# A two-layer mixture of experts in one kernel: second choices chained behind first choices, rows that carry the residual, and shared units moved between the lists

## The reference, cut

```python
x = x + gnn0(layernorm(x), adj)        # eigenvectors U of the 64 x 64 normalised Laplacian of adj
#   agg = U.T @ features; out = U @ (relu(agg @ W1 + b1) @ W2 + b2)
x = x + ffn0(layernorm(x))
#   probs = softmax(x @ router.T); top 2 of 8 experts, gates normalised
#   out = sum over both: gate_e * ((silu(x @ w1_e.T) * (x @ w3_e.T)) @ w2_e.T)     hidden 341
x = x + gnn1(layernorm(x), adj)
#   A_hat mixes the 64 nodes; relu(batchnorm(agg @ W1.T + b1)) @ W2.T + b2, batchnorm   hidden 256
x = x + ffn1(layernorm(x))
#   shared = gelu(x @ W1s + b1s) @ W2s + b2s                                       hidden 512
#   top 2 of 8: gate_e * (gelu(x @ W1p_e + b1p_e) @ W2p_e + b2p_e), plus shared    hidden 512
```

## Time and profile before

| what | value |
|---|---|
| median of three runs | 1467.68 us (1464.34 to 1473.49) |
| the profiled execution | 1468.22 us, span 1466.4 us |
| busy, share of the span | PE 77%, DVE 62%, POOL 45%, ACT 38% |
| mean granted TensorE clock | 0.922 |
| DMA over the span | 125.58 MB, mean 86 GB/s |
| first instruction of the experts to the last, layer 0 | 442.2 to 802.2 us |
| the same, layer 1 | 1093.3 to about 1431 us |

### The profile page before, as it was taken

The page is one execution under the profiler, slowest core; times in us unless marked ns, Lnnn a source line. Parts: engine busy times, 40 slices in busy tenths (PEclk is TensorE's granted clock), DMA queues, the critical chain, the costliest instruction groups (busy, mean ns, idle before and its releaser), DMA issues.

```text
span 1466.4 us, 24078 instructions
## 1 busy us (share of the span) xinstructions
PE 1125.4 (77%) x6500; PEld 934.2 (64%) x6500; DVE 902.9 (62%) x3796; ACT 550.2 (38%) x1613; POOL 653.2 (45%) x675
## 2 busy tenths in 40 slices
PE   4555686388727978899999677999878877799990
PEld 3555575266615856688888443776657766699990
DVE  5776789767763544456676778887614433355673
ACT  3556567045511211122222365554323322244440
POOL 3000000054566666665444840044546666656664
PEclk9999999999958998899999798899989988899995
DMA  9993000001112222222242600011112222222436
GB/s 230 428 427 146 1 1 1 0 1 34 37 48 70 72 63 62 64 65 60 84 119 70 229 18 15 5 34 33 39 45 66 68 62 64 62 68 70 131 104 229
DMA packets 59270, 125.58 MB, mean 86 GB/s; under 512 B 13132, under 2 KB 39637, under 8 KB 57600
## 3 DMA queue, kind: packets, MB, share of 16 engines
q0 software_dynamic: 20000, 73.21, 13.2%
q1 hardware_dynamic: 39136, 50.84, 12.9%
HBM read 50.83 MB, written 74.99 MB: 86 GB/s over the span
## 4 chain that ended last, share of the span: by engine, by line
PE 48%; issue 32%; another core or an unknown queue 7%; DVE 6%; ACT 2%; DMA 2%; SPq 2%; POOL 1%; DVEq 0%; POOLq 0%; ACTq 0%
PE bank L1619 15%; PE bank L1610 9%; PE bank L1608 6%; PE bank L1607 6%; PE bank L1828 3%; PE bank L1836 3%; PE bank L1787 2%; PE bank L1595 2%; DMA u<-planes 1%; DVE bnh L1684 1%; PE bank L861 1%; SPq L2148 1%; DVE bn L1123 1%; ACT pay L1903 1%
## 5 line engine op out<-in xcount | busy, mean ns | idle before, releaser
L1462 POOL DMA_INDIRECT planes<-work,goal x284 | 300.9, 1059 | 211.0 <-DVE work L1531 124.2
L1016 POOL DMA_INDIRECT rows<-pay,slot x256 | 257.7, 1007 | 245.4 <-issue 78.3
L1619 PE MATMUL bank<-pay 128*128 128x128 f32 (+1 forms) x1988 | 297.7, 290 | 66.1 <-issue 34.0
L1619 PEld LDWEIGHTS bank<-pay 128*128 128x128 f32 (+1 forms) x1988 | 272.4, 199 | 95.3 <-issue 44.4
L1579 ACT ACTIVATE pay<-bank,pay 128x256 f32<-128x256 f32 x284 | 127.1, 475 | 211.3 <-PE bank L1610 123.9
L1575 ACT ACTIVATE pay<-bank 128x256 f32<-128x256 f32 (+1 forms) x213 | 81.1, 383 | 301.7 <-PE bank L1608 224.1
L1610 PE MATMUL bank<-pay 128*128 128x256 f32 x568 | 145.5, 402 | 3.0 <-issue 1.6
L1552 DVE TENSOR_TENSOR pay<-pay,bank 128x256 f32<-128x256 f32 (+1 forms) x213 | 88.6, 418 | 86.6 <-ACT pay L1575 44.5
L1607 PE MATMUL bank<-pay 128*128 128x256 f32 (+1 forms) x426 | 134.2, 398 | 7.6 <-issue 7.0
L1608 PE MATMUL bank<-pay 128*128 128x256 f32 (+1 forms) x426 | 131.7, 392 | 0.0
L195 PE MATMUL bank<-u 63*64 63x2 f32 (+61 forms) x496 | 73.7, 255 | 67.2 <-DVE u L180 66.1
(11 more groups left out here) (416 smaller groups left out, 2013.2 us busy)
## 6 DMA issues: line engine op xcount, KB each, us to landing
rows<-pay POOLq DMA_DIRECT2D x10, 3432.0 KB, 56.3
pay<-rows SPq DMA_DIRECT2D x142, 130.0 KB
u<-planes SPq DMA_DIRECT2D x64, 256.0 KB, 5.0
planes<-work,goal POOLq DMA_INDIRECT x284
wreg<-in_w SPq DMA_DIRECT2D x1, 4264.0 KB, 24.4
wreg<-in_w SPq DMA_DIRECT2D x1, 4112.0 KB, 13.3
X<-in_x SPq DMA_DIRECT2D x2, 2048.0 KB, 20.0
rows<-pay,slot POOLq DMA_INDIRECT x256
```

Source lines behind the costliest of these rows:

```text
L1016: return self.nc.gpsimd.indirect_dma_start(out=xs, out_offset=bass.IndirectOffsetOnAxis(ap=self.t["slot"][:, k, q:q + 1], axis=0), in_=sel ...
L1462: nc.gpsimd.indirect_dma_start(out=planes, out_offset=bass.IndirectOffsetOnAxis(ap=t["goal"][:, j * 2 + h:j * 2 + h + 1], axis=0), in_=t[" ...
L1619: ins = T.matmul(ps[4 + j % 2][:, h * P:(h + 1) * P], t["hh"][c][0:n, h * P:(h + 1) * P], t["wst"][j % 2][0:n, at + c * P:at + (c + 1) * P ...
```

## The change

First and second choices become two lists of 36 tiles (`LIST`), which run one after the other. A row now carries more: 128 features of the residual `X`, the 128 normalised features, and four numbers (token's number, both gates, and the slot of the token's second choice in `rows`, `AT_NEXT`); 260 floats. `finish` adds the gated result to the residual in the row itself (in `xin`, a ring of eight). For the first list POOL sends the whole row on to the slot of the second choice; for the second list it sends the 128 features to the token's place in `plane` (layer 0) or directly in `out` (layer 1). The second list's slots are filled from the upper end of each expert's room downwards. So there are no second sends and no planes to add.

Each list has 25 pure tiles and 11 split ones, whose two halves of 128 rows may have different experts: two weight sets are copied, up-products are done by halves, ACT does two gelus for one. Weight buffers are four (`WAYS`). SP waits at the start of the second list until every row of the first has been returned. In layer 1 the last 16 shared units (`HELD` = 2 token tiles) run on PE between the lists, and `RATE` is 5. The shared result of the first eight token tiles (`EARLY`) is added to `X` before these are sent; for the other eight ACT keeps it (`keep_shared`), and after the lists only these eight are fetched from `out`, added and stored again. The zero fill is twice as large, 20 blocks, and the wait for it moves from DVE at the start of graph layer 0 to ACT ahead of the first row of `first_norm_apply`.

```diff
-NT = (2 * TOKENS + E8 * (TS - 1)) // TS
+PURE = -(-(TOKENS - E8 * (TS - 1)) // TS)
+MIXED = (TOKENS + E8 * (P - 1)) // P - 2 * PURE
+MIXED += MIXED % 2
+LIST = PURE + MIXED // 2
+SETS = PURE + MIXED
+NT = 2 * LIST
+NS = 2 * SETS
-ROW = P + 2
+ROW = P + 4
+AT_ID, AT_G2, AT_G1, AT_NEXT = range(P, P + 4)
+FULL = P + ROW
-BLOCKS = 10
-RING = 18
-ZERO = E8 * CAP * ROW // (P * BLOCKS)
+BLOCKS = 20
+RING = 8
+WAYS = 4
+ZERO = E8 * CAP * FULL // (P * BLOCKS)
...
     if q == 0:
         act.wait_ge(*E.at("l1_scale"))
+        act.wait_ge(S("cleared"), 16 * BLOCKS)
...
     V.tensor_copy(t["rows"], ps[6][:, 0:1]).then_inc(S("a0_rows_out"), 1)
-    dve.wait_ge(S("cleared"), 16 * BLOCKS)
...
     for j in range(NT):
-        if route.split and j == PURE:
-            sp.wait_ge(S("route_sent_second"), 16 * N * sum(SPLIT[:layer + 1]))
-        at = sp.value_load(t["first"][j:j + 1, 0:1], min_val=0, max_val=E8 * CAP - TS)
-        if j >= 4:
-            sp.wait_ge(s("t"), past("t", j - 3))
-            sp.wait_ge(s("goal"), past("goal", j - 3))
-            sp.wait_ge(s("ys"), past("ys", j - 3))
...
+        if j == LIST:
+            for r in range(RING):
+                sp.wait_ge(s(f"back{r}"), past(f"back{r}", 32 * uses(r, LIST)))
...
+        if j >= RING:
+            sp.wait_ge(s(f"back{j % RING}"), past(f"back{j % RING}", 32 * (j // RING)))
+        if split(j):
+            for h in range(2):
+                sp.dma_start(t["xin"][j % RING][:, h, :], xs[bass.ds(ats[h], P), :]).then_inc(s(f"xin{j % RING}"), 16)
+        else:
+            sp.dma_start(t["xin"][j % RING], xs[bass.ds(ats[0], TS), :].rearrange("(p h) c -> p h c", h=2)
+                         ).then_inc(s(f"xin{j % RING}"), 16)
...
+    for j in range(NT):
+        out, width, column, last = (xs, FULL, P + AT_NEXT, E8 * CAP - 1) if j < LIST else (result, P, P + AT_ID, TOKENS - 1)
+        if split(j):
+            pool.wait_ge(s("goal"), past("goal", splits_before(j) + 1))
         pool.wait_ge(s("ys"), past("ys", j + 1))
         for h in range(2):
...
             nc.gpsimd.indirect_dma_start(
+                out=out, out_offset=bass.IndirectOffsetOnAxis(ap=goal, axis=0), in_=t["xin"][j % RING][:, h, 0:width],
+                in_offset=None, bounds_check=last, oob_is_err=False).then_inc(s(f"back{j % RING}"), 16)
...
-            for q in range(FREE + k * SENDS, min(N, FREE + (k + 1) * SENDS)):
-                route.send(q, 1, xs).then_inc(S("route_sent_second"), 16)
-            if k >= BEHIND:
-                give_back(j)
-                j += 1
...
-        if j >= RING:
-            dve.wait_ge(s("freed"), past("freed", j - RING + 1))
-        V.tensor_tensor(t["ysb"][j % RING], y, gate, ALU.mult).then_inc(s("ys"), 1)
+        gate = P + (AT_G1 if j < LIST else AT_G2)
+        for h in range(2):
+            ins = V.scalar_tensor_tensor(out=row[:, h, 0:P], in0=y[:, h, :], scalar=row[:, h, gate:gate + 1],
+                                         in1=row[:, h, 0:P], op0=ALU.mult, op1=ALU.add)
+        ins.then_inc(s("ys"), 1)
...
+        if j + 1 == LIST:
+            finish(j)
...
+                if split(j):
+                    A.activation(t["hh"][c][:, 0:P], ps[c][:, 0:P], ACT.Gelu, bias=bias[0])
+                    A.activation(t["hh"][c][:, P:TS], ps[c][:, P:TS], ACT.Gelu, bias=bias[1]).then_inc(s("hh"), 1)
...
+        if layer == 1 and j == LIST - 1:
+            for n in range(AHEAD, UNITS):
+                shared_act(nc, act, S, t, ps, n)
+                if n % (2 * CH1) == 2 * CH1 - 1:
+                    keep_shared(nc, act, S, t, ps, n // (2 * CH1))
...
+        for k, set_no in enumerate(sets_of(j)):
+            w = t["wst"][set_no % WAYS]
+            to = slice(k * P, (k + 1) * P) if split(j) else slice(0, TS)
+            ins = T.matmul(ps[c][0:n, to], w[:, a:a + n], x[:, to], start=True, stop=True)
...
+        if j + 1 == LIST:
+            if layer == 1 and HELD:
+                pe.wait_ge(s("ys"), past("ys", LIST - 1))
+                for n in range(AHEAD, UNITS):
+                    shared_pe(nc, pe, S, t, ps, n)
+                pe.wait_ge(S("a1_kept"), TILES - EARLY)
+            turn_in(LIST)
...
+def fetch_rows(sp, S, t, result, layer, tiles):
+
+    for r in range(RING):
+        sp.wait_ge(S(f"tile_back{r}"), 32 * uses(r, NT) * (layer + 1))
+    for T in tiles:
+        qs = slice(T * PAIRS, (T + 1) * PAIRS)
+        sp.dma_start(t["X"][:, qs, :], result[:, qs, :]).then_inc(S(f"rows{layer}_{T}"), 16)
...
-RATE = 6
+RATE = 5
+EARLY = 8
+HELD = 2
 UNITS = 2 * CH1 * TILES
-A1_STEPS = 2 + -(-UNITS // RATE)
+AHEAD = UNITS - 2 * CH1 * HELD
+A1_STEPS = 2 + -(-AHEAD // RATE)
+IN_ORDER = (0, 1, 2, 4, 3, 5, 6, 7)
...
     def ready(g):
         pool.wait_ge(S("a1_xh"), GT * (g + 1))
+        if GT * g < EARLY:
+            pool.wait_ge(S("a1_xsh"), GT * (g + 1))
 
     def rest(g, k):
-        if g + 1 < GROUPS:
-            pool.wait_ge(S("a1_hh"), RATE * g + (13, 14, 16)[k - 1])
-    for g in range(GROUPS):
+        if GT * (g + 1) < EARLY:
+            pool.wait_ge(S("a1_hh"), CH1 * GT * (g + 1) + (1, 2, 4)[k - 1])
+    for g in IN_ORDER:
         route.scatter(pool, g, xs, ready, rest)
...
+LATE = range(EARLY, TILES)
...
-    for T in range(TILES):
+    for T in LATE:
         qs = slice(T * PAIRS, (T + 1) * PAIRS)
-        pool.wait_ge(S("late_add"), TILES + T + 1)
+        pool.wait_ge(S("whole"), T - EARLY + 1)
         pool.dma_start(out[:, qs, :], t["X"][:, qs, :]).then_inc(S("stored"), 16)
```

More of the change, by code:

```diff
@@ L826 @@
               picked=GROUPS, gates=GROUPS, total=1, limits=1, limit_row=1, first=1)
-SENT = [16 * N if split else 32 * N for split in SPLIT]
+SENT = 16 * N
 def due(s, lag):
@@ L910, in choose @@
         dve.wait_ge(own.sem, n)
[L911 to L914, removed]
+        n = 2 * E8 * GQ
+        marks, i, e = r["o"], r["i"], r["e"]
         n = own.inc(V.tensor_tensor_scan(i, self.K[:, K_RESET:K_RESET + n], marks, 0.0, ALU.mult, ALU.add))
@@ L1020, in all_sent @@
     def all_sent(self, eng):
[L1022 removed]
+        eng.wait_ge(self.s("sent"), SENT * (self.layer + 1))
     def table(self, dve, own):
[L1026 to L1031 removed]
@@ L1058, in table @@
-        own.chain(V.tensor_tensor_scan(end, self.t["ones"][:, 0:n], k, 0.0, ALU.mult, ALU.add))
-        own.chain(V.tensor_tensor(start, end, k, ALU.subtract))
-        own.inc(V.tensor_scalar(m, start, j, None, ALU.is_le))
-        if self.split:
-            own.chain(V.tensor_tensor(start, start, f, ALU.subtract))
-        own.chain(V.tensor_scalar(u, start, -float(TS), j256, ALU.mult, ALU.add))
-        own.chain(V.scalar_tensor_tensor(out=m, in0=end, scalar=j, in1=m, op0=ALU.is_gt, op1=ALU.mult))
@@ L1065, in table, with by_list @@
-        whole = each_part(count[:, n - E8:n])
-        own.inc(V.tensor_tensor(by_part(k), whole, by_part(u), ALU.subtract))
-        own.chain(V.tensor_tensor(by_part(u), by_part(u), base, ALU.add))
-        own.inc(V.tensor_tensor(k, k, m, ALU.mult))
+        V, K, s, tb = self.nc.vector, self.K, self.s, self.t["tb"]
+        count, a, cum = tb["count"], tb["a"], tb["cum"]
+        begin, end, u, m, w = (tb[name] for name in ("begin", "end", "u", "m", "w"))
+        def by_list(ap):
+            return ap.rearrange("p (l e) -> p l e", e=E8)
@@ new lines, in table @@
+        whole_begin, whole_end = by_kind(begin)[:, :, 0, :], by_kind(end)[:, :, 0, :]
+        half_begin, half_end = by_kind(begin)[:, :, 1, :], by_kind(end)[:, :, 1, :]
+        dve.wait_ge(s("total"), self.past("total", 1))
+        own.chain(V.tensor_tensor(count, self.total, base, ALU.subtract))
+        own.chain(V.tensor_tensor(cmp, count.unsqueeze(2).to_broadcast([P, 2 * E8, 32]), steps(K[:, K_WHOLE:K_WHOLE + 32]),
+                                  ALU.is_gt))
+        own.chain(V.tensor_reduce(a, cmp, AX.X, ALU.add))
@@ new lines, in table @@
+        own.inc(V.tensor_tensor(w, end, place, ALU.is_gt))
+        own.chain(V.tensor_tensor(u, place, begin, ALU.subtract))
+        own.inc(V.tensor_tensor(m, m, w, ALU.mult))
+        own.chain(V.tensor_tensor(u, u, size, ALU.mult))
+        own.chain(V.scalar_tensor_tensor(out=by_kind(u)[:, :, 1, :], in0=by_list(cum), scalar=float(TS),
+                                         in1=by_kind(u)[:, :, 1, :], op0=ALU.mult, op1=ALU.add))
+        own.chain(V.tensor_tensor(by_kind(w), by_list(count).unsqueeze(2).to_broadcast([P, 2, 2, E8]), by_kind(u), ALU.subtract))
@@ L1076, in table @@
-        if self.split:
-            self.second_slots(own, count[:, E8:2 * E8], one_base, tb["f"][:, 0:E8], tb["look"])
+            own.inc(V.tensor_reduce(self.t["expert"], m, AX.X, ALU.add))
+        own.chain(V.tensor_reduce(tb["v"], w, AX.X, ALU.add))
+        V.tensor_scalar(tb["diag"], self.t["ident"], tb["v"], None, ALU.mult).then_inc(s("limits"), 1)
         own.chain(V.memset(self.t["goal"], NOWHERE))
@@ L1921, in gnn1_act @@
         normalised(s)
+        for n in units(s - 1):
+            keep(n)
```

(2 more changed lines are left out.)

546 lines of the change are left out of this document (253 added, 293 removed).

## The result

The changed kernel takes 1410.37 us (median of four, 1407.57 to 1412.88), the kernel before 1470.55 (1464.34 to 1473.49) on the same chip: ratio 0.9596, 95% interval 0.9552 to 0.9639. The time lies in the stated range, 17 us above the forecast of 1393. On another chip the sign turns: there the changed kernel is 2.4% slower than the one before, and variants of it are 2.2 to 2.7% slower on two more.

A forecast was written before the change was run, and what follows sets the result against it. POOL's unbroken issue of indirect DMAs was taken to delay other engines' signals, making thin stretches (TensorE with gaps). Terms -33 -33 -6 -5 -1 +2 gave -76 (unrounded -75), hence 1393 us; range 1368 to 1450.

The forecast's parts named there:

- Layer 0: -33: Experts of layer 0: 327 us instead of 360, with 6.6 for split tiles, 13.5 between lists, 3 for the start.
- T: Time per tile in the expert stages, taken as unchanged: 4.22 us in layer 0, 3.74 in layer 1.
- Layer 1: -33: Experts of layer 1: 305 us instead of 337.6, with 11 for split tiles, 21.6 for held units, 3 for the start.
- Graph layer 1: -6: Graph layer 1: 16 units less, set against sends that lose their pacing; -6 us, bounds -14 and +8.
- I put +8: Graph layer 1: sends of groups 3 to 7 go out as eight indirect DMAs in a row, costing 8 us.
- the -14 for the units: Graph layer 1: 16 shared units fewer at 0.88 us each, a gain of 14 us.
- Start: +2: Zero fill of twenty blocks ends at about 214; ACT's first scaled row waits for it: +2 us (0 to +4).
- Mix and tail: -6: Tail -5 us, half of -10 lost to fetches in 512-byte pieces; mix -1, losing POOL's add.
- B: Expert stages: about 36 tiles stay late by a third of the former lateness; 1440 us (1415 to 1460), 21%.
- case A: Whole kernel: the main forecast of 1393 us holds, range 1370 to 1415; 62%.
- C: Expert stages: row traffic to DRAM, not POOL's pace, slows tiles; both first lists stay slow; 1536 us, 10%.
- D: Zero fill ends late, at 226, holding ACT and the eigenvalue steps by 14 us; 1405 us, 5%.

The follow-up runs named there:

- e3: Kernel before with POOL's catching up put off: one give-back per tile, two only from tile 37 on; 1485.85 us, 0.8% over before.
- e2: Changed kernel plus a third indirect DMA per tile in both expert stages: 1538.71 us without bytes, 1551.88 us with them.
- e8: Kernel before, unchanged, on a third chip, one without late signals; 1325.5 us.
- e11: Changed kernel with later-opening pauses between graph layer 1's sends, on the third chip; 1355.47 us, ratio 1.0255 to the kernel before.
- e9: Changed kernel, unchanged, on the third chip; 1355.12 us, ratio 1.0236 to the kernel before.
- e1: Changed kernel with pauses between all pairs of sends in graph layer 1, on a chip with late signals; 1396.68 us, ratio 0.9471.

## Why the prediction was right, and where it was not

**What bounds the kernel before: right for that chip, and only for it.** Late signals with POOL's unbroken issue were the excess, put at 131 us; on the chip without them the same two stages are 124 us shorter. e3 moves the stretch with POOL's queue, e2 makes it anew with near-empty transfers, and the changed kernel's tiles of 121 GB/s show none. That the changed kernel's own gain is the absence of these is shown by the chips without them: there the same change costs 33 us. A condition of the chip decides the sign. I had taken it for a property of every chip, and no rival held it; nothing in one profile could have told me. That the result came from a chip with this condition is luck, and so is part of the 17 us by which the total is off: graph layer and start are 34 and 9 us above their forecasts, layer 1 and mix with tail 13 and 10 below.

**Layer 0: -33, measured -33.6.** Its terms held too. Split tiles: 11 x (4.64 - 4.22) + 11 x (4.50 - 4.22) = 7.7, forecast 6.6. Turn of the lists: 14.18 + 5.98 for two periods in place of 8.44, 11.7, forecast 13.5. Start 2.9, forecast 3. The doubled cost of DVE's finish is covered, T is 4.22.

**Layer 1: -33, measured -45.6.** The split tiles cost 5 us in place of 11, the held units with entry and exit 17.1 in place of 21.6 (21.23 + 3.30 for two tiles, less 2 x 3.73), and the thin first tile (3) did not come. The unit's price of 1.36 us was read in a stretch of the graph layer where signals are late; the split tiles' 11 was a choice between 0 and 26.

**Graph layer 1: -6, measured +27.9.** This is the step that failed, in "*I put +8*" for the sends that lose their pacing, with +8 as the upper end of the layer. The mechanism was right, the size was not: the steps of 13.1, 14.8 and 23.1 us take 7.5, 6.1 and 7.8 on the chip without late signals, so a burst of eight costs 5.6 and 8.7 us and one of sixteen 15.3, and all 64 sends stand in such bursts, not only those of groups 3 to 7. Against that chip the layer of the kernel before is 23.3 us longer, that of the changed kernel 51.8: the lateness grew by 28.5, not by 8. The pauses kept for the first groups do not bite, because these groups now wait for the shared adds and open only when the gelus that they would pause for are done. And the -14 for the units is a bound that even a chip without late signals does not give: -0.6, the sends being the end of the layer.

**Start: +2, measured +11.3.** The fill is right: ACT waits till 214.90 instead of starting at 212.05, the graph layer starts 1.7 later. The other 9 us can't be put down to the change. In this pair the product of the counts of layer 0 comes 10.1 us later (431.2 against 421.1) and the new table's chain of small DVE operations runs 19.1 us from it to the product of its limits (at 450.3), where the old took 12.8 (to 433.9). But the same code varies as much between runs: the product stands at 422.5 to 432.1 in the other traces with the new routing, and at 421.3, 426.7 (e8) and 435.9 (e3) with the old. A part of it is TensorE's clock: from 292 to 340 us it is 0.96 in the profile before and 0.86 in the one after, and on one chip, with the same code up to there, 0.93 goes with a product at 422.5 (e11) and 0.86 with one at 429.4 (e9). What sets the clock there is open. The chain takes 10.0 us on the chip without late signals and 8.0 the old one, so about 2 us are the new table's own; that it took 19.1 here may be late signals, but e1 ran it in 10.2 on a chip that has them. The forecast of +2 is neither borne out nor refuted.

**Mix and tail: -6, measured -15.5.** The mix stage gave 5.5 rather than 1 (3.4 on the chip without late signals), and the half number of tiles in the tail gave its -10 in full: the pieces of token order took nothing back.

**The rivals.** B (part of the lateness stays, 1440) came in part: lateness stayed, but inside the graph layer, while B had put it on the tiles of the first lists, none of which is late. The time, 1410, lies at the upper edge of case A. C is refuted by e2 and e3. D did not come: the fill went on at 427 to 428 GB/s until 200 us, and its last landing is at 40.9 plus 173.9, that is 214.8. The 358 GB/s of the Trainium skill, page "DMA: Bandwidth & Descriptors", section Specifications, do not bound the one core that runs here: slices of the fill moved 427 to 429 GB/s again.

## What to carry to other kernels

In this case an idle time "until remote" after the producer had ended was time lost on the way of a signal. Before a kernel is rebuilt around it, run the unchanged kernel on other chips, since here the same program takes 1474 or 1322 us, and a change worth 4% on the one loses 2.4% on the other. Where POOL issues indirect DMAs, two for each tile of 4.22 or 3.73 us were safe on all chips used here, and pauses must be set against what has been reached when the queue opens, or they hold nothing. When a stage's last transfers come out of one engine's queue, work taken from another engine does not shorten it, as 16 units fewer gave 0.6 us in the graph layer of e9.

## What the runs showed of the hardware that was not expected

On one of the four chips of the experiments, and on that of the result (perhaps the same one), completion signals arrive some us late, 6.5 in the earlier trace rows, while POOL issues indirect DMAs without a pause (1.28 us each), even ones that move next to no data: 144 of them, 0.08 MB in 4608 packets, cost 129 us. On the other three chips nothing of it shows at the same density: not one of their eight profiles has an idle time "until remote", and the kernel before is 150 us faster. What differs between the chips no run here tells; each of the four was used at one time only, so a condition of the hour is not excluded either. Where signals are late, two DMAs per 4.22 us tile cost nothing, three some 0.7 us a tile in layer 0 (48.9 us over 72 tiles), and the thin stretch of the kernel before, at 0.62 POOL instructions per us against 0.56 in e2's layer 0, 1.8 us a tile.
